# Retention projections: from one fp32 product per tile to three fp32r products per pair of tiles, and last sums read back in two parts

## What is computed

```python
x = layernorm(x + L0_attn(x, ...))       # retention, 16 heads of 16
x = layernorm(x + L0_ffn(x, ...))        # ternary weights
x = layernorm(x + L1_attn(x, ...))
x = layernorm(x + L1_ffn(x, ...))        # 8 experts, 2 groups, capacity 160

# L0_attn (retention)
qkv = x @ W_qkv                          # 256 -> 3 x 256
q, k, v = split into 16 heads of 16
ret = einsum('bhtd,bhsd->bhts', q, k) * decay
r = einsum('bhts,bhsd->bhtd', ret, v) + einsum('bhtd,hde->bhte', q, past_kv) * 256
y = group norm of r per batch            # over all heads and tokens of the batch
```

## Time and profile before

| | us |
|---|---|
| median of 3 runs (895.0 to 896.32) | 895.27 |
| the profiled execution's own time | 892.54 |
| its span in the profile | 890.9 |
| TensorE busy | 815.3 (92%) |
| VectorE busy | 598.5 (67%) |
| ScalarE busy | 488.7 (55%) |
| GpSimd busy | 272.7 (31%) |

### The profile page before, as it was taken

How to read it: one execution, slowest core, us unless ns; L and a number is a source line. 1 busy time by engine, 2 the same in 40 slices (tenths; PEclk the granted TensorE clock), 3 DMA queues, 4 the chain that set the end, 5 groups by cost and what they waited for, 6 DMA issues and landing times. The chain is left out here.

```text
span 890.9 us, 23450 instructions
## 1 busy us (share of the span) xinstructions
PE 815.3 (92%) x8950; PEld 667.5 (75%) x8950; DVE 598.5 (67%) x1439; ACT 488.7 (55%) x1018; POOL 272.7 (31%) x335
## 2 busy tenths in 40 slices
PE   6999999998899999998999899998988879999960
PEld 5888888887677777766777688886655549999950
DVE  3677778778557777778555425577667886657627
ACT  2544443443777777775974244556575435454426
POOL 1257763221112222224000000124443134656344
PEclk9999999999999999999999999999999989999985
DMA  8600000000000000001478534435222314566439
GB/s 321 197 21 22 18 24 18 18 12 3 1 1 1 1 1 1 1 1 34 126 196 199 132 92 131 136 101 198 93 85 99 103 31 121 142 201 161 119 64 343
DMA packets 74637, 79.55 MB, mean 89 GB/s; under 512 B 21824, under 2 KB 65728, under 8 KB 74176
## 3 DMA queue, kind: packets, MB, share of 16 engines
q1 hardware_dynamic: 69584, 72.36, 26.6%
q0 software_dynamic: 3968, 5.25, 3.4%
q10 hardware_dynamic: 1008, 0.91, 0.3%
HBM read 50.70 MB, written 27.79 MB: 88 GB/s over the span
## 5 line engine op out<-in xcount | busy, mean ns | idle before, releaser
L729 DVE TENSOR_TENSOR r_prob<-r_pS,const 128x512 f32<-128x512 f32 x128 | 81.9, 682 | 24.7 <-PE r_pS L551 24.7
L1106 DVE SCALAR_TENSOR_TENSOR f_gl<-att_res,small_first,f_gh 128x512 fp32r<-128x512 f32 x64 | 47.3, 747 | 35.7 <-ACT f_gh L1031 33.4
L1685 POOL TENSOR_TENSOR att_res<-att_res,t_hy 128x1024 f32<-128x1024 f32 x8 | 15.5, 1958 | 165.2 <-DVEq L2182 165.2
L960 PE MATMUL f_pY<-wpjT,f_gh 128*128 128x256 f32 x256 | 65.4, 290 | 0.3 <-DVE f_gl L1106 0.3
L961 PE MATMUL f_pY<-wpjT,f_gl 128*128 128x256 f32 x256 | 62.7, 279 | 0.0
L1374 PEld LDWEIGHTS q_bank<-q_xT,att_res 128*64 128x64 f32 x1024 | 57.3, 140 | 7.2 <-issue 4.2
L1374 PE MATMUL q_bank<-q_xT,att_res 128*64 128x128 f32 x1024 | 60.9, 279 | 0.0
L960 PEld LDWEIGHTS f_pY<-wpjT,f_gh 128*128 128x128 f32 x256 | 48.1, 188 | 15.9 <-issue 13.4
L2595 POOL DMA_INDIRECT sum_dram<-e_yo,y_id x24 | 43.1, 1795 | 54.6 <-ACT e_yo L2732 39.5
L1025 ACT ACTIVATE att_res<-f_pH 128x512 f32<-128x512 f32 x64 | 38.0, 594 | 38.6 <-PE f_pH L945 37.8
L2713 ACT ACTIVATE e_hh<-e_pH 128x320 fp32r<-128x320 f32 x64 | 26.2, 433 | 54.0 <-PE e_pH L2637 53.8
(11 more groups left out here) (336 smaller groups left out, 2350.6 us busy)
## 6 DMA issues: line engine op xcount, KB each, us to landing
kv_dram<-att_res SPq DMA_DIRECT2D x32, 256.0 KB, 3.5
t_ring<-kv_dram SPq DMA_DIRECT2D x128, 64.0 KB, 2.3
wi<-L_ffn_wi SPq DMA_DIRECT2D x8, 1024.0 KB, 5.0
wo<-L_ffn_wo SPq DMA_DIRECT2D x8, 1024.0 KB, 7.6
x_res<-L_attn_x SPq DMA_DIRECT2D x8, 512.0 KB, 7.0
q_dram<-att_res SPq DMA_DIRECT2D x16, 256.0 KB, 3.5
t_q<-q_dram SPq DMA_DIRECT2D x8, 512.0 KB, 4.4
x_dram<-x_res SPq DMA_DIRECT2D x8, 512.0 KB, 3.0
```

The lines of the kernel that those rows point to most:

```text
L729: dve.tensor_tensor(prob[t % 2][:, r, :, :], pS[r][:, :, :], dec[:, r, :, :], ALU.mult)\
L960: pe.matmul(out, gh[c % 4][:, cols], net.wpjT[:, c, :], start=(c == 0 and t % 2 == 0), stop=False, skip_group_check=True)
L1106: dve.scalar_tensor_tensor(out=gl[c % 4][:, :], in0=g[c][:, :], scalar=net.lnw[:, c:c + 1], in1=gh[c % 4][:, :], op0=ALU.mult, op1=ALU.sub ...
```

## The change

**Retention.** Queries and keys are computed for two tiles at once (256 columns), into one bank `pQK`, keys first, then queries. Weights `w` and tiles `xT` are split into a high part (fp32r, copied by ScalarE: `wh`, `xh`) and the rest (`wl`, `xl`, by VectorE for the weights and the second pair, by GpSimd's `low_x` for every later pair), and each product is made of three: high by high, high by low, low by high. The first pair of batch 0 stays fp32. Values are still made tile by tile, also from three products, and now stand behind the scores of the tile before. ScalarE has the masked copies of the queries once a pair (`take_queries`), behind the copy of the values of the next tile. The x tiles lie in pairs with 256 columns, and the wait for the first product is for both tiles of the pair. Later x tiles are loaded when their pair has been split.

**End.** For the last expert the row tiles go in the order 0, 2, 1, each in a bank of its own; r = 1 has its own semaphore `last_stored`, and only the read-back of batches 4 to 7 waits for it. A partition holds four rows that follow each other in DRAM, 4 KB, in place of four rows 128 apart.

```diff
-    xT = [sb(f"xT{i}", [P, KD, P]) for i in range(TPB)]
+    xT = [sb(f"xT{j}", [P, KD, 2 * P]) for j in two]
...
-    pQV = ps("pQV", [P, 512])
-    pKK = ps("pKK", [P, 512])
+    pQK = ps("pQK", [P, KD, 2, P])
+    pVK = ps("pVK", [P, 512])
...
         def next_turned(b, t):
-            sp.wait_ge(kT_made.sem, kT_made.after(b * TPB + t + 1 - TPB))
+            j = t // 2
+            if isinstance(b, int) and b == 1 and j == 0:
+                sp.wait_ge(v_made.sem, v_made.after(2))
+            else:
+                sp.wait_ge(x_split.sem, x_split.after(2 * b + j - 2))
...
+        def low_x(b, j):
...
+            pool.wait_ge(high_ready.sem, high_ready.after(2 * b + j + 1))
+            pool.tensor_tensor(xl[j][:, :, :], xT[j][:, :, :], xh[j][:, :, :], ALU.subtract).then_inc(x_split.sem, 1)
...
+        def take_queries(b, j):
+            act.wait_ge(qk_made.sem, qk_made.after(2 * (2 * b + j) + 2))
+            act.wait_ge(r_made.sem, r_made.after(b * TPB + 2 * j + 2 - TPB))
+            nc.scalar.activation(qT2[j][:, :, :, :].rearrange("p t k n -> p k t n"), pQK[:, :, :, :], ACT.Copy)
+            for odd, mask in enumerate(("even", "odd")):
+                ins = nc.scalar.activation(qEO2[j][:, :, :, odd, :].rearrange("p t k n -> p k t n"), pQK[:, :, :, :], ACT.Copy, scale=net.table[mask])
+            ins.then_inc(q_copied.sem, 1)
...
         def batch(b, before, behind):
             for t in range(TPB):
+                if t % 2 and behind:
+                    high_x(b + 1, t // 2)
                 if t + 1 < TPB:
                     take(b, t + 1)
                 elif behind:
                     take(b + 1, 0)
+                if t == 1:
+                    take_queries(b, 1)
+                elif t == 3 and behind:
+                    take_queries(b + 1, 0)
                 if t == 1 and before:
                     normed(b - 1)
...
+        def keys_of(b, j):
+            q = 2 * b + j
+            pe.wait_ge(x_split.sem, x_split.after(q))
+            pe.wait_ge(q_copied.sem, q_copied.after(q))
+            project(b, j, DIM, pQK)
+
+        def queries_of(b, j):
+            pe.wait_ge(k_taken.sem, k_taken.after(2 * b + j + 1))
+            project(b, j, 0, pQK)
...
+                terms = [(wh, xh[j]), (wh, xl[j]), (wl, xh[j])]
...
-                if t + 1 < TPB:
-                    project(b, t + 1)
-                elif behind:
-                    project(b + 1, 0)
+                if t < 2 or behind:
+                    (keys_of, queries_of)[t % 2](*((b, 1) if t < 2 else (b + 1, 0)))
...
                 scores(b, t, before)
+                if t + 1 < TPB:
+                    values_of(b, t + 1)
+                elif behind:
+                    values_of(b + 1, 0)
                 if last:
                     mix(*last)
...
-    sum_rows = net.sum_dram.rearrange("(b t p) d -> b p t d", p=P, t=TPB)
-    out_rows = net.out.rearrange("b (t p) d -> b p t d", p=P)
+    sum_rows = net.sum_dram.rearrange("(b p t) d -> b p t d", p=P, t=TPB)
+    out_rows = net.out.rearrange("b (p t) d -> b p t d", p=P)
...
-            sp.wait_ge(stored[p].sem, stored[p].after(48 * EXPERTS // 2))
+            sp.wait_ge(stored[p].sem, stored[p].after(48 * EXPERTS // 2 - 16 * p))
         for b in range(BATCH):
+            if b == BATCH // MGROUPS:
+                sp.wait_ge(last_stored.sem, last_stored.after(16))
             sp.dma_start(net.x_res[:, of(b), :], sum_rows[b]).then_inc(sum_in[b].sem, 16)
...
-            for r in range(3):
+            for r in range(3) if e < EXPERTS - 1 else (0, 2, 1):
                 send_rows(e, r)
```

More of the change, by code:

```diff
@@ L287, in retention @@
     small_in, small0_in, later_in = sig("small_in"), sig("small0_in"), sig("later_in")
-    x_in, x_full = [sig(f"x_in{t}") for t in range(TPB)], sig("x_full")
+    x_in, x_full = [sig(f"x_in{j}") for j in two], sig("x_full")
+    high_ready, x_split = sig("high_ready"), sig("x_split")
     fc_in, pj_in = sig("fc_in"), sig("pj_in")
@@ L366, in decay_queries @@
             i = b * TPB + t
-            pool.wait_ge(q_copied.sem, q_copied.after(i + 1))
+            pool.wait_ge(q_copied.sem, q_copied.after(2 * b + t // 2 + 1))
             pool.wait_ge(r_made.sem, r_made.after(i + 1 - TPB))
@@ L389, in gpsimd @@
         for t in range(TPB):
+            if t % 2:
+                low_x(1, t // 2)
             decay_queries(0, t)
@@ L399, in gpsimd, with batch @@
         pool.wait_ge(steps.sem, steps.done(1))
-        def batch(b):
+        def batch(b, behind=True):
             for t in range(TPB):
+                if t % 2 and behind:
+                    low_x(b + 1, t // 2)
                 decay_queries(b, t)
@@ L411, in gpsimd @@
             batch(b)
-        with pool.Fori(5, BATCH) as b:
+        with pool.Fori(5, BATCH - 1) as b:
             steps.enter(b - 5, 5)
             batch(b)
-            steps.leave(BATCH - 5)
+            steps.leave(BATCH - 6)
+        batch(BATCH - 1, False)
         group_pow(BATCH - 1)
@@ L494, in scalar @@
         nc.scalar.activation(vO[0][:, 0:1], vO[0][:, 0:1], ACT.Copy)
+        act.wait_ge(w_in.sem, w_in.after(16))
+        nc.scalar.activation(wh[:, :, :], w[:, :, :], ACT.Copy).then_inc(high_ready.sem, 1)
+        high_x(0, 1)
+        take_queries(0, 0)
         take(0, 0)
@@ L533, in project @@
                     pe.wait_ge(ks_ready.sem, ks_ready.after(turned))
-            for m in range(2):
-                for k in range(KD):
-                    mm = pe.matmul(pKT[:, m, :], w[:, k, DIM + m * P:DIM + (m + 1) * P], xT[t][:, k, :],
-                                   start=(k == 0), stop=(k == KD - 1))
-            mm.then_inc(kT_made.sem, 1)
+            if isinstance(b, int) and 2 * b + j == 0:
+                terms = [(w, xT[0])]
+            else:
+                terms = [(wh, xh[j]), (wh, xl[j]), (wl, xh[j])]
+            terms = [(ws, xs, k) for ws, xs in terms for k in range(KD)]
+            for n, (ws, xs, k) in enumerate(terms):
+                mm = pe.matmul(pV, xs[:, k, mine], ws[:, k, 2 * DIM:], start=(n == 0), stop=(n == len(terms) - 1))
+            mm.then_inc(v_made.sem, 1)
         def scores(b, t, before):
             i = b * TPB + t
-            pe.wait_ge(qv_taken.sem, qv_taken.after(i + 1))
-            pe.wait_ge(k_taken.sem, k_taken.after(i + 1))
+            pe.wait_ge(q_copied.sem, q_copied.after(2 * b + t // 2 + 1))
+            pe.wait_ge(k_taken.sem, k_taken.after(2 * b + t // 2 + 1))
             pe.wait_ge(s_taken.sem, s_taken.after(4 * i))
@@ L812, in batch @@
             for t in range(TPB):
-                if t + 1 < TPB:
-                    take(b, t + 1)
-                elif behind:
+                if t == 0:
+                    take(b, 1)
+                elif t == 2 and behind:
                     take(b + 1, 0)
@@ L838, in batch @@
                     norm_rows(b - 1, j)
+        low_parts()
+        take(0, 0, first_keys)
         norm_parts()
-        take(0, 0)
         batch(0, False, True)
@@ L2730, in body @@
                 else:
-                    act.wait_ge(d_made.sem, d_made.after(2 * e + r + 1))
-                nc.scalar.activation(yo[p][0:n, r, :], back(r), ACT.Copy, scale=net.slot_gate[0:n, r, bass.ds(e, 1)]).then_inc(d_act.sem, 1)
+                    act.wait_ge(d_made.sem, d_made.after(2 * e + r // 2 + 1))
+                nc.scalar.activation(yo[p][0:n, r, :], back(r) if behind else last_back(r), ACT.Copy, scale=net.slot_gate[0:n, r, bass.ds(e, 1)]).then_inc(d_act.sem, 1)
             if behind:
@@ L2802, in body @@
                 wi_part(e + 1, 1 - p)
-            dve.wait_ge(d_made.sem, d_made.after(2 * e + 2))
+            dve.wait_ge(d_made.sem, d_made.after(2 * e + (2 if behind else 3)))
             if behind:
```

123 lines of the change are left out of this document (73 added, 50 removed).

## The result

The changed kernel takes 913.03 us (median of 4 runs, 911.53 to 914.44) against 895.13 (4 runs, 894.42 to 896.32): a ratio of 1.0198, 95% interval 1.0178 to 1.0219, or 17.9 us more. The forecast was 901.3, between 890 and 908. The sign was right, the size was not.

A forecast was written before the change was run, and what follows sets the result against it. The prediction took TensorE, busy in all of a 20 us retention window, as the bound. Start +8.0, six loop batches +1.5, last batch +0.9 and end -4.4 gave +6.0 on the 895.27 median: 901.3 us, range 890 to 908.

The forecast's parts named there:

- First wait 0.8: Loop batch, tile 2: TensorE waits 0.8 us ahead of the keys for ScalarE's masked copy of the queries.
- third wait 0.6: Loop batch, tile 3: the queries' copies hold up the keys of the next second pair by 0.6 us.
- the landing of tile 1: Start: tile 1 of x lands at 13.5 us and the first product starts there, 6.3 us late.
- 51 of each per us: Start: SyncE's and ScalarE's queues alternate packet by packet, so packet count, not bytes, sets landing; 112 more packets, 2.2 us.
- TensorE saves 2.2 us a batch: Loop: projections take 8.8 us a batch, format changes included, in place of 11.0.
- GpSimd's two new differences a batch: Loop: GpSimd's low-part subtractions, some 1.3 us each, lie beside the path at no cost.
- The rest of batch 0: Start, after the first scores: waits and late fetching of the next batch's tiles lose 1.3 us, between 0 and 3.
- Last batch: +0.9: Last batch: less TensorE work against a 2.8 us wait for `r_taken` and late turned keys; +0.9 us, between -1 and +1.5.
- Row tile 1's DMA lands before the fifth read-back is wanted: End: row tile 1's indirect DMA delays no read-back, within an end term of -4.4 us.
- (a): Rival: loop waits are absent, copies covered, TensorE stays the bound; -12.4 us, 883; chance 0.12.
- (b): Rival: loop waits are half as long, 1.2 us a batch; -3.4 us in all, 892; chance 0.15.
- (d): Rival: VectorE also becomes the bound, idling longer for turned keys; 1 us more a batch, 907 or above; chance 0.08.

The follow-up runs named there:

- e5: Changed kernel with ScalarE copying the queries ahead of the values in tiles 1 and 3; 902.61 us, ratio 1.0107 to the kernel before.
- e7: Changed kernel with the turned inputs stored by pairs in DRAM, one DMA of 2 KB packets per pair; ratio 1.0177 to the kernel before.
- e6: Changed kernel with GpSimd's low-part difference cut to 4 of 256 columns from the second batch on (timing only); 910.66 us, ratio 1.0196.
- e8: Changed kernel with its pairs and order, but each product made once in fp32, without high and low parts; 913.98 us, ratio 1.0223.
- e9: e5 with GpSimd making the second pair's low part only once the carried state is done; 896.83 us, ratio 1.0022 to the kernel before.
- e2: Kernel before with only the end's order 0, 2, 1 and the read-back in two parts, rows of 1 KB; ratio 0.9984.
- e3: Kernel before with only the end's 4 KB rows, all scatters waited for before any read; ratio 0.9999.
- e4: Changed kernel with its end as in the kernel before, retention keeping all of the change; 914.73 us, ratio 1.0229.
- e12: e11 with 4 KB rows and the wait for row tile 1's DMA ahead of the third read; ratio 0.9925 to the kernel before.
- e10: e9 plus pair rows, first batch's first scores ahead of its second pair's keys, and the end of e2; 889.45 us, ratio 0.9929.
- e11: e10 plus six idle products in the last batch and VectorE copying second-pair keys ahead of turned keys in the first; 887.02 us, ratio 0.9913.

## Why the prediction was right or wrong, point by point

**Right.** The direction, and ScalarE's order as its cause. "First wait 0.8" and "third wait 0.6" are 0.8 and 0.6 in the trace, the second 0.4 for 0.6, and e5 shows that they are this order: turning it round gives back 1.4 us a batch. The wait of 2.8 us in the last batch is 2.57.

**Right in kind, near by luck: the landing of tile 1.** It is 12.4 for a forecast of 13.5, and e7, with a quarter of the packets and the same bytes, has 7.9, so it is not the bytes that set it. But "51 of each per us" is not how it came about: ScalarE's queue began 1.5 us later than in e7 and then moved 251 packets in one microsecond, and these two deviations pull in opposite directions. The rule of the Trainium skill (DMA: Bandwidth & Descriptors, Queues, rings and completion order), by which the tiles would land at about 8 us, did not give the time in the changed kernel either.

**The loop: "A batch needs 48 for queries and keys and 24 for values, 8.4 us, and I add 0.05 for each of 8 changes of format, 8.8. … TensorE saves 2.2 us a batch."** This term was mis-sized and is the largest error. The groups take 4 x (1.52 + 0.91) = 9.7 us. A product in the middle of a group is 0.12 us, as the earlier trace rows had it; 72 of them are 8.6, and the rest is (9.7 - 8.6) / 8 = 0.14 us for each group in the mean (0.1 for a group of 12, 0.2 for a group of 6), three times what was put for a change of format. TensorE saves 1.3, not 2.2: 0.9 us a batch, 5.4 in six.

**The loop: "GpSimd's two new differences a batch … lie beside all this."** This step failed. They lie beside VectorE and slow it: e6 and e8, without them, have its busy time at 21.2 and 20.9 us a batch for 22.7 after, and e9 removes the wait for the state by moving one of them. The sum had 0.4 for all lateness of VectorE; the wait costs 0.96. By the measured terms a batch is 0.8 + 0.4 + 0.6 + 1.0 = 2.8 us of waits less 1.3 saved, +1.5; by the period it is +1.3, for a forecast of +0.25.

**The start: "The rest of batch 0 loses by the waits told next and because the next batch's tiles are fetched only when tile 1's values are made: I put 1.3, between 0 and 3."** From the first scores of batch 0 to those of batch 1 are 29.95 us for 24.40: 5.6, outside my bounds. The scores of tile 0 themselves are 6.1 late for a forecast of 6.7. This step failed. I had the late fetch and not the order of SyncE's queue, in which the pair's second tile stands behind two loads of `x_res` rows, while ScalarE now waits for the whole pair. It waits 6.35 us, TensorE then twice, and the clock falls. With pair rows, the pair ahead of those rows, the same stretch is 26.2: 3.8 of the 5.6 hang on this load and on the clock, which did not fall in e7. 1.2 hang on ScalarE's order (e5).

**Last batch: +0.9.** The waits were sized rightly: without the clock's fall the stretch is 26.0 to 26.1, 0.8 to 0.9 over before. The fall adds 1.6 in most traces; the forecast had no clock in it.

**The end: "Row tile 1's DMA lands before the fifth read-back is wanted."** This step failed. It gave this DMA no length and no price for the reads beside it; the only row shown, 3.27 us, is the DMA of row tile 2, with half the rows and no read beside it. Row tile 1's took 3.8 before and 7.6 among four reads, and the last four read-backs waited. The parts are near their numbers one at a time, -2.0 (e2) for -2.7 and -1.3 (e3) for -1.7, and together -0.4 to -2.7, by how long this DMA takes. The larger packets do raise the rate: 418 to 422 GB/s in the windows of 2 us from 900 to 908, for 347 to 385 in those from 872 to 888 before.

The rivals (a) and (b), shorter waits, are out. (d), VectorE as a bound "as well", was the nearest in time, but its mechanism (idle time for turned keys) is not the one that came: VectorE was made slower.

What stays open: why the clock falls behind some idle stretches and not behind others of the same length; what makes row tile 1's DMA take 6.7 in one trace and 8.3 in another; what part of pair rows' gain is packets and what part is the place in the queue, and by how much they shorten the timed median.

## What to carry to other kernels

Moving a product behind another moves its copies behind everything that the copying engine has queued, so write out that engine's order first and put the copies whose reader comes first in front; here turning it round was worth 8.5 us in six batches and 1.2 in the first. Work "beside" the path on GpSimd is not free when VectorE's operations on SBUF run at the same time: give it a moment in which VectorE reads PSUM or has slack, and when a transfer is put beside another, price it by a row in which it has company. Whenever a tile in SBUF becomes part of a wider one, count the packets of each queue, and look at what stands in the queue between the parts that are now waited for together.

## What the runs showed of the hardware

- GpSimd's 128x512 subtraction slowed VectorE by kind of operation. The state's (two inputs in SBUF) took 350 ns in the median before and 578 after, the 128x1 product L851 (L771 before) 158 and 636; the masks of the scores (one input in PSUM) 682 and 682. The Trainium skill (GPSIMD Engine Reference, Specifications) names contention for operations with two inputs in SBUF or in a 2-port mode; the trace agrees on the first. The 128x2 scaling L849 (L769 before), with one tile as input, went from 169 to 696 ns in the mean too; whether it ran in such a mode no run shows.
- The indirect DMA of row tile 1 with accumulation (128 rows): 3.7 to 3.8 us when no read-back ran beside it (before, e3, e4), 5.9 beside two (e12), 6.4 to 6.6 beside four of 1 KB rows (e2, e10, e11), 6.7 to 8.3 beside four of 4 KB rows. Row tile 2's (64 rows), with no read-back beside it: 3.1 to 3.3.
- ScalarE's DMA queue, with tiles of 256 packets of 512 bytes at its head, moved its first packet at 5.5 us and then 251 packets in a microsecond in which SyncE's moved 80; later both moved 111 in 2 us.
- An fp32r product of 256 columns is 0.12 us within a group; a group of 12 takes 0.1 us more, one of 6 0.2. Four fp32 products of 256 columns take 1.73 us, the twelve of fp32r in their place 1.52.
- Behind an idle stretch of 1.8 or 2.6 us in the last batch TensorE's granted clock fell to 1.2 GHz in six of eight traces, at a cost of 1.6 us, and stayed at 2.4 GHz in two.
